# Three rounded passes in place of full fp32 products in the attention of a token model

## The reference

```python
h = concat(token_table[ids], cat_table[ids])           # 64 x 128 x 256
def attn(x):                                           # x = layernorm(h)
    qkv = (x @ W_qkv + b_qkv).reshape(b, s, 3, H, D)   # 256 x 768, 16 heads of 16
    pq, pk = elu(q) + 1, elu(k) + 1
    kv = einsum('bshd,bshm->bhmd', pk, v)
    z = 1 / (einsum('bshd,bhd->bsh', pq, pk.sum(axis=1)) + 1e-6)
    return einsum('bshd,bhmd,bsh->bshm', pq, kv, z)
h = h + attn(layernorm(h))
def ffn(x):                                            # x = layernorm(h)
    rw = gating(x)                                     # 16 experts, two or so per token, softmax over them
    q, k, v = [einsum('btc,ech,bte->bth', x, w, rw) for w in (q_proj, k_proj, v_proj)]
    ao = causal_softmax(q k^T / sqrt(128)) v
    return einsum('bth,ehc,bte->btc', ao, o_proj, rw)
h = h + ffn(layernorm(h))
```

## Time and profile before

| what | value |
|---|---|
| median of 3 runs | 1187.47 us (1186.08 to 1189.19) |
| the profiled execution | 1176.88 us, span 1175.0 us |
| PE busy | 1029.2 us (88%) |
| PE weight loads | 862.2 us (73%) |
| DVE busy | 928.9 us (79%) |
| ACT busy | 533.6 us (45%) |
| POOL busy | 754.4 us (64%) |
| the token stage | phi of the first tile at 33.87 us, of the last at 442.30 us |
| the sorted stage | first row loads at 478.46 us, last product at about 686 us |

### The profile page before, as it was taken

The page is one execution under the profiler, slowest core; times in us unless marked ns, Lnnn a source line. Parts: engine busy times, 40 slices in busy tenths (PEclk is TensorE's granted clock), DMA queues, the critical chain, the costliest instruction groups (busy, mean ns, idle before and its releaser), DMA issues.

```text
span 1175.0 us, 26735 instructions
## 1 busy us (share of the span) xinstructions
PE 1029.2 (88%) x6571; PEld 862.2 (73%) x6572; DVE 928.9 (79%) x3134; ACT 533.6 (45%) x1455; POOL 754.4 (64%) x975
## 2 busy tenths in 40 slices
PE   1999999999999993599999959999999999999898
PEld 0565656565666662588988849999999889988897
DVE  3789999999999996245544528999888888888898
ACT  3544444444433431234443425555555555555554
POOL 6657777777777756700000037888888888888785
PEclk9999999999999995799999979999999999999999
DMA  5642333333222225576777752333333333333230
GB/s 141 201 151 88 100 104 99 104 95 100 77 86 86 80 75 197 180 231 221 239 223 232 224 177 77 95 91 91 90 90 89 89 89 89 89 89 89 85 93 32
DMA packets 108096, 143.28 MB, mean 122 GB/s; under 512 B 15388, under 2 KB 95330, under 8 KB 107876
## 3 DMA queue, kind: packets, MB, share of 16 engines
q1 hardware_dynamic: 88004, 91.17, 24.4%
q0 software_dynamic: 18880, 50.36, 15.0%
q10 hardware_dynamic: 1152, 1.05, 0.3%
HBM read 77.37 MB, written 72.46 MB: 128 GB/s over the span
## 4 chain that ended last, share of the span: by engine, by line
PE 40%; DVE 22%; POOL 18%; issue 13%; ACT 3%; DMA 2%; POOLq 1%; SPq 0%; DVEq 0%; ACTq 0%
PE bank L1366 8%; PE bank L1291 7%; PE bank L1293 7%; PE bank L1292 7%; PE bank L1298 5%; POOL row_y L747 5%; POOL qk_neg L732 2%; POOL x2T L732 2%; PE bank L1364 2%; DVE phi L1055 2%; POOL x2T L728 2%; POOL x2T L734 2%; POOL qk_neg L728 2%; DVE h L1075 1%; POOL sorted_x L674 1%
## 5 line engine op out<-in xcount | busy, mean ns | idle before, releaser
L1291 PE MATMUL bank<-wo_hi,split_lo 128*128 128x256 f32 x1024 | 302.8, 296 | 4.6 <-DVE qk_e L1228 2.2
L1292 PE MATMUL bank<-wo_lo,split_hi 128*128 128x256 f32 x1024 | 287.3, 281 | 0.0
L1293 PE MATMUL bank<-wo_hi,split_hi 128*128 128x256 f32 x1024 | 287.2, 280 | 0.0
L1291 PEld LDWEIGHTS bank<-wo_hi,split_lo 128*128 128x128 f32 x1024 | 194.5, 190 | 9.3 <-DVE qk_e L1228 4.6
L1366 PE MATMUL bank<-w_attn,x1T 128*128 128x512 f32 (+1 forms) x512 | 201.2, 516 | 0.0
L1292 PEld LDWEIGHTS bank<-wo_lo,split_hi 128*128 128x128 f32 x1024 | 194.5, 190 | 0.0
L1293 PEld LDWEIGHTS bank<-wo_hi,split_hi 128*128 128x128 f32 x1024 | 194.0, 189 | 0.0
L843 ACT ACTIVATE h<-bank,rwo 128x256 f32<-128x256 f32 x256 | 107.4, 471 | 126.8 <-PE bank L1293 99.5
L747 POOL DMA_INDIRECT row_y<-sorted_y,pair_now x128 | 128.4, 1003 | 36.3 <-issue 28.5
L1166 DVE TENSOR_TENSOR split_lo<-bank,split_hi 128x256 fp32r<-128x256 f32 x144 | 61.2, 425 | 104.2 <-ACT split_hi L812 103.0
L740 POOL COPY pair_now<-pair_at 128x2 uint32 (+1 forms) x64 | 13.1, 205 | 195.7 <-SPq L531 195.6
(11 more groups left out here) (223 smaller groups left out, 2516.0 us busy)
## 6 DMA issues: line engine op xcount, KB each, us to landing
sorted_y<-row_y SPq DMA_DIRECT2D x36, 384.0 KB, 3.1
sorted_y<-w_attn SPq DMA_DIRECT2D x36, 384.0 KB, 3.2
row_x<-sorted_x SPq DMA_DIRECT2D x72, 128.0 KB, 2.4
h_rows<-h SPq DMA_DIRECT2D x64, 128.0 KB, 1.8
row_x<-h_rows SPq DMA_DIRECT2D x64, 128.0 KB, 2.9
out_h<-row_x SPq DMA_DIRECT2D x64, 128.0 KB, 2.0
category_table<-in_L_tok_special_table SPq DMA_DIRECT2D x10, 623.0 KB, 5.0
phi<-sorted_x SPq DMA_DIRECT2D x36, 128.0 KB, 2.1
```

The lines of the kernel that those rows point to most:

```text
L1291: pe.matmul(ps, left[1][c], right[0][c], start=(c == 0), stop=False)
L1292: pe.matmul(ps, left[0][c], right[1][c], start=False, stop=False)
L1293: last = pe.matmul(ps, left[0][c], right[0][c], start=False, stop=(c == n - 1))
```

## The change

The attention products (`attn_product`) are now done as three rounded passes, as the other products are: rows and weights are each split into a rounded part and a remainder, and remainder times rounded, rounded times remainder and rounded times rounded are added. For this ACT's `x1_T` copy writes the rounded type, a new DVE operation `x1_lo` per tile subtracts it from the turned tile in PSUM, and the attention weights are split once, at the start, by ACT and DVE. The space for the split attention weights is that of the output weights, which are free only after the token stage. So the output weights' sixteen quarters are loaded and split in steps -8 to 7 of the sorted stage. The q, k and v quarters stay in the token stage, two to each step from -7 to -1 and one to each from 0 to 33.

```diff
 P1_STEPS = [...
-            "x1_normed", "x1_turned", "x1_T", "qk_product", ...
+            "x1_normed", "x1_turned", "x1_T", "x1_lo", "qk_product", ...
+        w_attn_s = [w[:, :, :].rearrange("p e c -> p (e c)")[:, 0:CH * 3 * C].rearrange("p (c n) -> p c n", c=CH)
+                    for w in wo]
+        x1T_s = [w[:, :, :].rearrange("p c t -> p (c t)") for w in split[0]]
         def weights_at(i):
             if -7 <= i < 0:
-                return range(4 * (i + 7), 4 * (i + 8))
-            n = 28 + i
-            return [n] if n < 4 * E else []
+                return range(2 * (i + 7), 2 * (i + 8))
+            n = 14 + i
+            return [n] if 14 <= n < 3 * E else []
+        def o_weight_at(i):
+            return 3 * E + i.c + 8 if i.j is None and -8 <= i.c < 8 else None
+        def load_weight(sp, n):
+            if n >= N_RAW:
+                sp.wait_ge(weights_lo, n - N_RAW + 1)
+            if n >= 3 * E:
+                src = o_proj[n - 3 * E]
+            else:
+                src = (q_proj, k_proj, v_proj)[n % 3][n // 3].rearrange("(c p) h -> p c h", p=P)
+            sp.dma_start(like(n), src).then_inc(raw_loaded[n % N_RAW], 16)
+        def weight_hi(act, n):
+            act.wait_ge(raw_loaded[n % N_RAW], 16 * (n // N_RAW) + 16)
+            act.copy(quarter_of((wq[0], wo[0]), n), like(n)).then_inc(weights_hi, 1)
+        def weight_lo(dve, n):
+            dve.wait_ge(weights_hi, n + 1)
+            dve.tensor_tensor(quarter_of((wq[1], wo[1]), n), like(n), quarter_of((wq[0], wo[0]), n).bitcast(F32),
+                              ALU.subtract).then_inc(weights_lo, 1)
...
 # SP, sorted stage
                 def step2(i):
+                    if o_weight_at(i) is not None:
+                        load_weight(sp, o_weight_at(i))
                     tile = i.shift(8)
...
 # ACT
             act.copy(ones_r[:, :], ones[:, :]).then_inc(setup_a, 1)
+            act.wait_ge(attn_loaded, 16)
+            act.copy(w_attn_s[0], w_attn[:, :, :]).then_inc(setup_a, 1)
...
-                    act.copy(x1T[:, :], ps_x1[:, 0:C]).then_inc(done["x1_T"], 1)
+                    act.copy(x1T_s[0], ps_x1[:, 0:C]).then_inc(done["x1_T"], 1)
...
                         act.copy(y_buf[i.c % 8 // 4][:, i.q, :], ps_y[i.q][:, 0:Y]
                                  ).then_inc(done["pair_copied"], 1)
+                    if o_weight_at(i) is not None:
+                        weight_hi(act, o_weight_at(i))
...
 # DVE
             def step1(i):
+                if i.c == -5:
+                    dve.wait_ge(setup_a, 4)
+                    dve.tensor_tensor(w_attn_s[1], w_attn[:, :, :], w_attn_s[0].bitcast(F32), ALU.subtract
+                                      ).then_inc(setup_v, 1)
...
                                       ).then_inc(done["attn"], 1)
+                if x1_tile.inside(B):
+                    after(dve, "x1_T", x1_tile)
+                    dve.tensor_tensor(x1T_s[1], ps_x1[:, 0:C], x1T_s[0].bitcast(F32), ALU.subtract
+                                      ).then_inc(done["x1_lo"], 1)
+                if attn_tile.inside(B):
                     after(dve, "attn", attn_tile)
...
                         dve.tensor_copy(y_buf[i.c % 8 // 4][:, i.q, :], ps_y[i.q][:, 0:Y]
                                         ).then_inc(done["pair_copied"], 1)
+                    if o_weight_at(i) is not None:
+                        weight_lo(dve, o_weight_at(i))
...
 # PE
-                    after(pe, "x1_T", tile.shift(-1))
+                    after(pe, "x1_lo", tile.shift(-1))
                     after(pe, "x1_normed", tile)
...
                     pe.matmul(ps[:, 0:hi - lo], ones_r[0:BIAS_ROWS, :], bias[:, lo:hi], start=True, stop=False)
+                    turned = [halves(x) for x in x1T_s]
                     for c in range(CH):
-                        last = pe.matmul(ps[:, 0:hi - lo], halves(x1T)[c], w_attn[:, c, lo:hi], start=False,
-                                         stop=(c == CH - 1))
+                        for x, w, end in ((1, 0, False), (0, 1, False), (0, 0, c == CH - 1)):
+                            last = pe.matmul(ps[:, 0:hi - lo], turned[x][c], w_attn_s[w][:, c, lo:hi], start=False,
+                                             stop=end)
                     last.then_inc(done[name], 1)
                 if tile.inside(B):
                     after(pe, "phi", tile.shift(-1))
-                    after(pe, "x1_T", tile)
+                    after(pe, "x1_lo", tile)
...
             def sorted_way():
-                pe.wait_ge(weights_lo, 4 * E)
+                pe.wait_ge(weights_lo, 3 * E)
...
             branch(pe, sorted_way, dense_way)
+            pe.wait_ge(weights_lo, 4 * E)
             pe.wait_ge(y_ready, 1)
```

More of the change, by code:

```diff
@@ L52 @@
 P1_STEPS = ["ln1_stats", "ln1_moments", "ln2_stats", "ln2_moments", "var_eps", "var_inv", "roots_in", "roots",
-            "x1_normed", "x1_turned", "x1_T", "qk_product", "v_product", "qk_negative", "qk_exp", "v_copied",
+            "x1_normed", "x1_turned", "x1_T", "x1_lo", "qk_product", "v_product", "qk_negative", "qk_exp", "v_copied",
             "phi", "phi_q_turned", "kv_product", "phi_q_T", "kv_masked", "attn_sums", "attn_den", "attn_z",
@@ L443, in quarter_of @@
         def quarter_of(split_weights, n):
-            e, part = n // 4, n % 4
-            if part == 3:
-                return split_weights[1][:, e, :]
+            if n >= 3 * E:
+                return split_weights[1][:, n - 3 * E, :]
+            e, part = n // 3, n % 3
             return split_weights[0][:, e, :, part * HD:(part + 1) * HD]
@@ L479, in step1 @@
                 for n in weights_at(i.c):
[L480 to L486, removed]
+                    load_weight(sp, n)
                 tile = i.shift(2)
@@ L533, in dense_way @@
             def dense_way():
+                for e in range(E):
+                    load_weight(sp, 3 * E + e)
                 rest = sorted_y[B * P:PAIR_TILES * P, :].rearrange("r y -> (r y)").rearrange(
@@ L799, in step1 @@
                 for n in weights_at(i.c):
-                    act.wait_ge(raw_loaded[n % N_RAW], 16 * (n // N_RAW) + 16)
-                    act.copy(quarter_of((wq[0], wo[0]), n), like(n)).then_inc(weights_hi, 1)
+                    weight_hi(act, n)
             run1(act, step1)
@@ L819, in step2 @@
                                  ).then_inc(done["pair_copied"], 1)
+                    if o_weight_at(i) is not None:
+                        weight_hi(act, o_weight_at(i))
                 run2(act, step2)
             def dense_way():
+                for e in range(E):
+                    weight_hi(act, 3 * E + e)
                 def token_tile(t, first):
@@ L1105, in step1 @@
                 for n in weights_at(i.c):
-                    dve.wait_ge(weights_hi, n + 1)
-                    dve.tensor_tensor(quarter_of((wq[1], wo[1]), n), like(n),
-                                      quarter_of((wq[0], wo[0]), n).bitcast(F32), ALU.subtract
-                                      ).then_inc(weights_lo, 1)
+                    weight_lo(dve, n)
             run1(dve, step1)
@@ L1173, in step2 @@
                                         ).then_inc(done["pair_copied"], 1)
+                    if o_weight_at(i) is not None:
+                        weight_lo(dve, o_weight_at(i))
                 run2(dve, step2)
             def dense_way():
+                for e in range(E):
+                    weight_lo(dve, 3 * E + e)
                 def token_tile(t, first):
@@ L1354, in step1 @@
                     if tile.c == 0:
-                        pe.wait_ge(setup_v, 6)
+                        pe.wait_ge(setup_v, 7)
                     for c in range(CH):
@@ L1371, in step1 @@
                     after(pe, "phi", tile.shift(-1))
-                    after(pe, "x1_T", tile)
+                    after(pe, "x1_lo", tile)
+                    if tile.c == 0:
+                        pe.wait_ge(setup_v, 6)
                     attn_product(ps_qk, 0, 2 * C, "qk_product")
```

3 lines of the change are left out of this document (2 added, 1 removed).

## The result

The changed kernel takes 1198.07 us (median, 1194.09 to 1209.73); measured beside it the kernel before takes 1188.11. The ratio over the runs is 1.0109, 95% interval 1.0069 to 1.0149 (1.0084 by the medians alone): slower, by 10.0 us by the medians. The profiled execution took 1197.07 us, its span is 1195.3.

A forecast was written before the change was run, and what follows sets the result against it. DVE, which never waits, was taken to bound the token stage, PE the sorted stage. Ramp -4.8, 58 periods +8.2 and sorted start +6.5 gave +9.9 us on 1187.5: 1197.4 us, range 1188 to 1213.

The forecast's parts named there:

- The products on PE: Token stage, q/k and v products: 3.61 us a tile becomes 2.45, relieving PE of about 1.15, worth nothing where DVE sets pace.
- x1_lo, +0.20 a period, +11.6: New DVE subtraction between attn and h2: 0.66 us where they took 0.46, so +11.6 us over the 58 token-stage periods.
- Waits that go and splits, -3.4: 58 token-stage periods: DVE's waits for the exponential go, -2.7 us, and fewer weight splits in the loop, -0.7.
- The ramp, -4.8: First token tiles, before the phi at 64.88 us: -4.8 us in all, from only -2 up to -8.
- steps a and b: Ramp: two splits fewer before the first x1, -0.7 us; a shorter first q/k product, -1.2, with x1_lo ahead of it, +0.4.
- steps c and d: Ramp: next three periods lose six splits, -2.0 us, gain three x1_lo, +0.6; last two lose 1.17 us waits, gain x1_lo, -1.9.
- The start, 6.0 to 6.8: Sorted stage's start: first copy of turned rows stands behind casts of weights 0 to 5, so 6.0 to 6.8 us late.
- Steps 0 to 7, 0 to 1: Sorted stage, steps 0 to 7: a further 0 to 1 us may be lost, where each weight load follows a store.
- Rival B: Token stage: the new subtraction costs its whole length, not overlapped or waiting for the cast; +15 us more, 1212; chance 0.14.
- C: Rival: the sorted stage's start is hidden, weights landing in 2 us and row loads passing them; +3.4, 1191 us; chance 0.12.
- D: Rival: TensorE sets the token stage's period after all, each falling by 1.1 us; -64 us, so 1125; chance 0.08.
- E: Rival: PE, busy some 78%, falls to its lower clock in the token stage; +200 us and more, 1400; chance 0.03.

The follow-up runs named there:

- lo_once: Changed kernel with the remainder of the rows formed for tile 0 alone, later tiles multiplying that stale one: 1183.66 us, ratio 1.0015 to the kernel before.
- only_moved: Kernel before with its full fp32 products and no x1_lo, but the expert weights in the changed kernel's places: 1188.21 us beside 1177.68, ratio 1.0081.
- double_lo: Changed kernel with a second, useless subtraction of the same operands right behind x1_lo: 1212.99 us beside the kernel before at 1182.25, ratio 1.0262.
- two_passes: Changed kernel without the pass rounded rows times remainder of the weights: 1194.46 us beside the kernel before at 1177.68, ratio 1.0154.
- the second run: Changed kernel measured and profiled once more, nothing edited: 1186.53 us beside the kernel before at 1177.68, ratio 1.0075.
- f32_eight_late: Kernel before, full fp32 products and no x1_lo, with eight output weights loaded and split late, in the sorted stage's first steps: 1182.30 us beside 1182.36, ratio 0.9995.

## Why the prediction was right, and where it wasn't

The forecast, 1197.4 us (+9.9), came out at 1198.07 (+10.0), and from its mechanism: DVE sets the token stage's pace and PE's relief isn't seen. But several terms of the sum were mis-sized, and that it still holds within 1 us is partly luck: the 58 periods were put 3.8 us too high and the start 1.1 to 1.3, the ramp's gain was put 1.0 to 1.7 us too large, and the steps after the start at least 1.0 us too low.

- *The products on PE, "relieved of about 1.15 us a tile".* Measured 0.46: 2.02 us for q and k instead of 2.33 and 1.13 instead of 1.28. I had multiplied the steady pace by the number of matmuls; from the bias to the first pass it takes 0.43 and 0.32 us, and the first pass 0.33 and 0.23. In the tiles with weight splits the miss changes nothing, since DVE sets the period there.
- *x1_lo, +0.20 a period, +11.6.* Right where it stands (0.34 + 0.33 - 0.46 = 0.21). Over the period it is 0.13 to 0.20 with the weight splits, and 0.15 after them (`lo_once`), which what falls away there just pays for.
- *Waits that go and splits, -3.4: the 58 periods, +8.2.* Measured +4.4 undisturbed. Missing was the shorter `roots_in`, some 2 to 2.5 us; the rest is the mean of 0.16 with the splits in place of 0.20. In the first profile the four slow periods brought it to +9.4.
- *The ramp, -4.8.* Measured -3.1 to -3.8. The first phi came 1.0 to 2.1 us earlier (1.5 by steps a and b), but the five periods up to the sixth gained only 1.6 to 2.2 where steps c and d have 3.3. Step d failed: the wait before phi did not go, it went from 1.17 us to 0.51, and the last ramp periods from 6.37 to 5.91. That is 0.46, PE's relief as measured. Here, where PE sets the pace, the mis-sized relief did cost the sum something. `only_moved`, without the relief, has its sixth phi at 65.00: fewer splits alone bring nothing.
- *The start, 6.0 to 6.8.* Measured 5.2 to 5.4, by the list that I had written out: weight 5 is cast right before the first copy. *Steps 0 to 7, 0 to 1.* Measured 2.0 to 3.2, the larger miss: I had counted SP's store ahead of each load, but not that ACT's cast in the same step waits for the landing.
- *The low end of the range, "+0.6".* By its own terms it is -8 + 8.2 + 3 = +3.2, so 1191 and not 1188. The result does not hang on it.
- *, "79% busy with the granted clock at 1.00".* Misread. The window reaches 3 us past the last product, so that the share is an average of work and of a stage that is over. Up to there PE was over 90% busy, and the row says nothing about a PE that is busy 79%:

```profile
670.00:686.00 16.00, 14.78 (x90) 13.75 (x90) 7.11 (x16) 6.30 (x16) 0.00 (x0) 1.00 0.72 239
686.00:690.00 4.00, 0.93 (x6) 0.60 (x4) 0.56 (x1) 0.48 (x1) 0.00 (x0) 1.00 0.58 207
```

Rival B fell: the first subtraction costs 0.21 in its place and the second, in `double_lo`, 0.32 to 0.35, where B has 0.46. C fell by the 8.2 us, D by `lo_once`, whose periods with splits are the old ones. E, against which the earlier trace rows is no evidence, came true in a small way. PE, busy 87% and not 78%, lost part of its clock in the token stage. The price is a few microseconds and not 200, since the granted clock over it is 0.92 to 1.00 and not 0.5, and several periods with 0.75 are no longer than their like. In `two_passes` it outweighs the pass saved.

What stays open: why the tables take 3.4 us on one chip and over 10.9 on others, in the same code; what makes a ramp period take 8.4 us in some profiles; and how much of the changed kernel's wider spread (15.6 us over four executions, 5.3 over six in the second run, 3.1 over four for the kernel before) is the clock. Of the four the slowest has the lowest mean granted clock, 0.951, and the fastest the highest, 0.966. No version here beats the kernel before. The one that ties with it, `f32_eight_late`, has its products. Three passes need an operation per tile for the remainder, here on the engine that is full; to give it to ACT or POOL was not tried.

## What to carry to other kernels

Taking work off an engine that is busy 92% is worth nothing while another, busy 94%, never waits; what counts is the one operation added to that other's queue, at its start-to-start price between its own neighbours. Work moved out of a full stage lands in another stage's queues: list what each in-order engine then issues ahead of the first useful instruction, and issue loads some steps ahead of the cast that waits for them. And profile both kernels twice, on the same chip, before a difference between two profiles is put down to an edit: here 8 of 20 us were not the edit's. Before a busy share is read, see that its window does not reach past the end of the stage.

## What the runs showed of the hardware that was not expected

- PE made slower by less work: the two-pass kernel has less to do on PE than the three-pass kernel, the lower granted clock (0.90 against 0.97 to 0.99) and the longer time. A busy share alone doesn't tell: in the same stretch, 145 to 280 us, PE is busy 82% in `two_passes` with 0.90 and 83% in `double_lo` with 0.97.
- A chain of rounded matmuls has a price at its head: 0.43 us from a bias matmul of 33 rows to the first pass and 0.33 for that pass, then 0.23 for each further one of 512 columns.
- The same few DVE operations on small tables took 3.4 to 3.5 us in five of the profiled executions and 10.9 to 14.1 in eight, with gaps of 1.1 to 1.3 us in front of them in the one shown. The four on chip 11 are all short, the seven on chips 5 and 7 all long.
- A DVE operation of two columns, 0.17 us alone, took up to 0.42 when it started 0.53 us or more into POOL's indirect DMA instruction of 0.97 to 0.99 us; it then ended 0.02 to 0.04 us before that instruction did.
